# Layer 2's attention: products in column halves except the scores, five score banks, projections of four head pairs tile by tile, and new orders

## The chip, the cores and the metric

The program runs on one NeuronCore of a Trainium2 chip. Five engines work side by side, each through its own queue in order, and hand work over by semaphores: TensorE (PE; its weight loads are shown apart, as PEld), VectorE (DVE), ScalarE (ACT), GpSimd (POOL) and SyncE (SP), which starts transfers here. TensorE writes into PSUM, eight banks of 128 partitions x 512 f32 numbers. The metric is the device time of one execution in microseconds (us).

## The reference

Four layers of attention and feed-forward on x of 8 x 512 x 128, each with a layer norm before and a residual added behind. The change touches only the attention of layer 2 (16 heads of 64, S = 512):

```python
q = jnp.einsum('bsd,hpd->bhsp', x, q_w) + q_b      # x is the layer norm's result
k = jnp.einsum('bsd,hpd->bhsp', x, k_w) + k_b
v = jnp.einsum('bsd,hpd->bhsp', x, v_w) + v_b
scores = jnp.einsum('bhqp,bhkp->bhqk', q, k) / jnp.sqrt(jnp.float32(P))
attn = jax.nn.softmax(scores, axis=2)              # over the queries q, not the keys
ctx = jnp.einsum('bhqk,bhkp->bqhp', attn, v)
out = concat(ctx) @ l_w.T + l_b                    # and x = x + out
```

Since the softmax runs over the queries, its sum belongs to a key, and the kernel divides the values by it instead of the exponentials.

## The kernel before

Every engine has one list of steps for this stage, a string of letters in `Attention2.ORDER`; `order()` turns a letter and its running number into a step. The letters that matter: a `vproj`, b `kq`, c `score`, d `ctx`, e `project`, f `turn`, g `ahead` (small work for the next layer), and on DVE also h `stats`, i `low parts`, j `rows`, k `values`, l `turned`, m `add`; on ACT o `ctx out`. An engine does its steps in that order and waits on semaphores inside them. Nothing else orders the work.

The work is cut into 64 units n: block b = n // 8 of 512 tokens (one sequence), and head pair hp = n % 8. For each unit:

- `kq` (L1973), twice: keys and queries of both heads, 128 x 512, from three f16 products (high x high, low x high, high x low: `PARTS`). ACT writes the high part into `T` (L2079), DVE the low part (L2033).
- `score` (L1994), four times, one for each tile j of 128 keys: three f16 products for each of the two heads. A head has 64 rows of contraction, so the two heads use the upper and lower row half of the array ("64*128" in the profile) and write two neighbouring banks. DVE takes the row maximum of both banks at once (L2048, 1024 elements) and scales it (L2050); ACT takes two exponentials into `E` with their sums (L2087, followed by a readout of the accumulator). 
- `values`: DVE inverts the sums (L2053), POOL multiplies the values by them into `vn` (L2109).
- `ctx` (L2004), twice, each for two key tiles: f32 products with 64 columns of weights for each head, so the two heads use the left and right column half of the array ("128*64"). `ctx out` (L2095): ACT copies the bank to `cx`.
- `project` (L2014): four f32 products of 128 tokens into bank 6, which sums over the eight head pairs of a block. After the eighth, DVE adds the bank to x (`add`, L213).

`vproj` (L1983) makes the values of a block, eight pieces of 128 x 512, with three f16 products each (DVE L2041 evacuates). `kq`, `vproj` and `project` use the whole array ("128*128").

An f32 product is two MATMUL records in the trace (x8 for four products), an f16 product is one.

PSUM: banks 0 to 3 hold two scores (score j uses banks 2(j % 2) and the next), so a score waits for both exponentials of the one two before it. The other uses rotate over banks 4, 5 and 7: `self.bank` numbers them in the order of the tensor list, and `released` lets a use wait until the third before it has been evacuated. Bank 6 is the projection's. `E` has six buffers (three units), `cx` two, `T`, `vn`, `mx`, `zs` two units each.

At its start the stage still shares DVE with the layer norms of later blocks (`stats`, `rows`: L161, L164, L179). At its end the next layer waits for the last `add`.

Of the kernel before, what the change touches and what calls it, by code (L numbers as in the profile page):

```python
# [7 lines left out]
ALU = mybir.AluOpType  # L8
# [1698 lines left out]
class LowRank:  # L1707
# [45 lines left out]
    def vector(self, v):  # L1753
# [40 lines left out]
        for n, b in enumerate((0, 1, ORDER[0])):  # L1794
            v.wait_ge(k.sem("x5"), b + 1)
# [57 lines left out]
class Attention2:  # L1853
# [4 lines left out]
    def __init__(self, k, pre, low, ctx):  # L1858
# [4 lines left out]
        self.E = [loc(f"E{i}", [128, 4, 512]) for i in range(6)]  # L1863
# [3 lines left out]
        self.cx = [loc(f"cx{i}", [128, 512]) for i in range(2)]  # L1867
        uses = [u for what, x in self.order("tensor") for u in self.banks(what, x)]
        self.bank = {u: (4, 5, 7)[i % 3] for i, u in enumerate(uses)}
        self.last = {u: uses[i - 3] for i, u in enumerate(uses) if i > 2}  # L1870

    PARTS = ((0, 0), (1, 0), (0, 1))

# [6 lines left out]
            "aaaaaaaabbbbccabbacccbccbcdcdcabcbecdcdcabcbedccdcacbbecdcdcabcbecdcdcabcbecdcdcfacbecbdcdcabcbecdcdcabcbecdcd"  # L1880
            "cabcbecdcdcabcbecdcdcabcbecdcdcggacbbcdcedcacbbecdcdcggfcabecbcdcdcabcbecdcdcggcabbcdcedccabbecdcdcggacbbcdced"
            "ccabbecdcdcggacbbcdcedcabcbecdcdcfacbecbcddccabbecdcdcabcbecdcdcabcbecdcdcabcbecdcdcabcbecdcdcabcbecdcdcabcbec"
            "dcdcfacbecbdcdcabcbecdcdcabcbecdcdcabcbecdcdcabcbecdcdcabcbecdcdcabcbecdcdcabcbecdcdcfacbecbdcdcabcbecdcdcabcb"
            "ecdcdcabcbecdcdcabcbecdcdcabcbecdcdcabcbecdcdcabcbecdcdcfacbecbdcdcabcbecdcdcabcbecdcdcabcbecdcdcggggggggggggg"
            "gggacbbecdcdcabcbecdcdcabcbecdcdcabcbecdcdcabcbecdcdcgggggbcbecdcdcbbcdcecdcbbcdcecdcbbcdcecdcbbcdcecdcbbcdcec"
            "dcdcecdcdcecdedde"),
        "vector": (
            "hhaaaaaaaahhiiijiccajjjhahccihhcckihcjcjjjickicachhciickhcacjjjjhhhccikiccahhciickhhcacjjjcijckihcacjjjcjihcki"
            "caclhciihckhcacjjjcjickicacmciickcacciickcacciickcacciickcnaccickiccaciickcncalcickiccacickiccncaickicmccackii"
            "ccnacickicccackiiccnacgggggggggggckgciicacggickicggccalckiciggggccaggckiicgcacmickicggcacggickicgcacgickicgggc"  # L1890
            "acgckiiccacickiccacickiccaclickiccacickiccacmickiccacickiccacickiccacickiccacickiccacickiccaclickiccacickiccac"
            "mickiccacickiccacickiccacickiccacickiccacickiccaclickiccacickiccacmickiccacickiccacgigckiccacickiccacickiccaci"
            "ckiccacickicccickicccickicmccickicccickicccickicccickicccckccckm"),
# [12 lines left out]

    def steps(self):
# [8 lines left out]
        every["add"] = range(NB)  # L1918
# [8 lines left out]

    def banks(self, what, x):

        if what in ("kq", "vproj"):  # L1930
            return [(what, x)]
# [15 lines left out]
    def evacuated(self, p, use):  # L1947
# [15 lines left out]
    def tensor(self, p):  # L1963
        k, ps, pre, vn, E = self.k, self.k.ps, self.pre, self.vn, self.E
        ahead = self.low.tensor(p, self.bank, self.released)
        for what, x in self.order("tensor"):
            if what == "kq":
# [4 lines left out]
                for o, (q, r) in enumerate(self.PARTS):  # L1972
                    t = p.e.matmul(ps[:, self.bank[what, x], :], pre.part(("kw", "qw")[x[1]], r, slice(128 * hp, 128 * hp + 128)), halves(k, b)[q],  # L1973
                                   start=o == 0, stop=o == 2)
                t.then_inc(k.sem("kqm").h, 1)
            elif what == "vproj":
# [5 lines left out]
                for o, (q, r) in enumerate(self.PARTS):  # L1982
                    t = p.e.matmul(ps[:, self.bank[what, x], :], halves(k, b)[q][:, 128 * j:128 * j + 128],  # L1983
                                   pre.part("vw", r, slice(512 * c, 512 * c + 512)), start=o == 0, stop=o == 2)
                t.then_inc(k.sem("vproj").h, 1)
            elif what == "score":
                n, j = x
                t, at = self.T[n % 2], 2 * (j % 2)
                p.wait_ge(k.sem("E"), 2 * (4 * n + j) - 2)
                p.wait_ge(k.sem("thi"), 2 * n + 2)  # L1990
                p.wait_ge(k.sem("tlo"), 2 * n + 2)
                for o, (q, r) in enumerate(self.PARTS):
                    for hh, rows in enumerate((slice(0, 64), slice(64, 128))):
                        y = p.e.matmul(ps[:, at + hh, :], t[rows, q, 128 * j:128 * j + 128], t[rows, 2 + r, :], start=o == 0, stop=o == 2)  # L1994
                y.then_inc(k.sem("score").h, 1)
            elif what == "ctx":
# [863 lines left out]
```

## Time and profile before

| | us |
|---|---|
| median of 3 runs | 1479.46 (1477.49 to 1480.4) |
| span of the profiled execution, first to last instruction | 1470.9 |
| PE busy in it | 1406.0 (96%) |
| DVE busy | 1191.3 (81%) |
| ACT busy | 1106.2 (75%) |
| POOL busy | 284.1 (19%) |

The page gives no time of its own for the profiled execution beside the span; the median of the runs is 8.6 us above the span, which is what lies around the first and last instruction. The attention of layer 2 fills the stretch from about 567 to 1220 us of the span. Durations are those of this one execution. The end of a matmul is modelled, so times of TensorE are best read from start to start: the start of a row minus the start of the next row is what the piece took of the engine.

### The profile page before, as it was taken

To read this page: it belongs to the slowest core of one execution; us is meant where nothing else is said; L and a number is where in the kernel's file an instruction comes from. 1 tells how busy PE (TensorE), PEld (TensorE's weight loads), DVE (VectorE), ACT (ScalarE), POOL (GpSimd) and SP (SyncE) were. 2 spreads that over 40 slices of the span, in tenths; PEclk is the share of its full clock that TensorE was granted. 3 is DMA by queue.
4 is the path that set the end of the run, shared out by engine and by line. 5 is a ranking of instruction groups with operands and counts; after the bars stand their busy time and mean duration, and the time that the engine had idled before them with its cause. 6 is when DMAs were issued, how large, how long until landed. Compare 5 with 4: busy or idle time off the path is not lost.

```text
span 1470.9 us, 23734 instructions
## 1 busy us (share of the span) xinstructions
PE 1406.0 (96%) x8601; PEld 680.8 (46%) x8601; DVE 1191.3 (81%) x2559; ACT 1106.2 (75%) x2072; POOL 284.1 (19%) x239
## 2 busy tenths in 40 slices
PE   5989999999989998999999999999999999999997
PEld 4643333332248875333333333333333335555796
DVE  7699768583369979998788998888788767999997
ACT  3579888898867733788788888888888885887645
POOL 6212000000023322221111110111011112243542
PEclk9999999999999999999999999999999999999999
DMA  4176555656210001000000000000000000000000
GB/s 109 28 156 179 155 146 153 150 147 153 100 55 2 1 1 72 1 1 1 1 1 0 1 1 1 1 1 1 1 1 1 1 30 1 1 8 8 8 15 23
DMA packets 43621, 63.15 MB, mean 43 GB/s; under 512 B 5360, under 2 KB 25072, under 8 KB 43120
## 3 DMA queue, kind: packets, MB, share of 16 engines
q1 hardware_dynamic: 43504, 61.62, 15.7%
q8 instruction: 69, 1.13, 0.3%
q14 instruction: 48, 0.39, 0.1%
HBM read 54.27 MB, written 7.34 MB: 42 GB/s over the span
## 4 chain that ended last, share of the span: by engine, by line
PE 73%; DVE 15%; POOL 3%; ACT 3%; issue 2%; DMA 2%; SPq 1%; DVEq 0%; ACTq 0%
PE ps L2004 16%; PE ps L1994 13%; PE ps L525 8%; PE ps L515 7%; PE ps L1973 6%; PE ps L2014 4%; PE ps L1983 3%; DVE p6ac L2504 2%; PE ps L534 2%; POOL WA L2184 1%; PE ps L2397 1%; DVE X L213 1%; POOL WA L2188 1%; DVE st L161 1%; PE ps L448 1%
## 5 line engine op out<-in xcount | busy, mean ns | idle before, releaser
L2087 ACT ACTIVATE p4E<-ps,p4mx,p4sc 128x512 f32<-128x512 f32 x512 | 393.6, 773 | 108.3 <-DVE p4mx L2050 107.7
L2048 DVE TENSOR_REDUCE p4mx<-ps 128x2 f32<-128x1024 f32 x256 | 312.7, 1222 | 86.8 <-PE ps L1994 84.2
L2004 PE MATMUL ps<-p4E,p4vn 128*64 128x512 f32 x1024 | 248.3, 606 | 0.2 <-POOL p4vn L2109 0.2
L1994 PE MATMUL ps<-p4T 64*128 64x512 f16 x1536 | 209.9, 380 | 5.9 <-ACT p4E L2087 5.9
L2109 POOL TENSOR_TENSOR p4vn<-p4v,p4zs 128x512 f32<-128x512 f32 x64 | 66.8, 1044 | 480.3 <-DVE p4zs L2053 480.3
L752 ACT ACTIVATE p1g<-ps,WB 128x1024 f32<-128x1024 f32 x128 | 135.7, 1118 | 17.9 <-PE ps L515 17.8
L657 DVE SCALAR_TENSOR_TENSOR p1Pb<-ps,WB,p1GB 128x512 f32<-128x512 f32 x128 | 94.9, 748 | 64.1 <-PE ps L525 60.7
L515 PE MATMUL ps<-p1R,p1w1s 128*128 128x512 bf16 x512 | 131.7, 381 | 6.7 <-ACT xT L752 4.5
L1994 PEld LDWEIGHTS ps<-p4T 64*128 64x128 f16 x1536 | 54.6, 94 | 174.9 <-issue 102.9
L525 PE MATMUL ps<-p1g,WB 128*32 128x512 f32 x512 | 125.7, 599 | 0.8 <-DMA p1GB<-gscr 0.7
L525 PE MATMUL ps<-xn,WB 128*32 128x512 f32 x256 | 124.8, 599 | 0.0
L2004 PEld LDWEIGHTS ps<-p4E,p4vn 128*64 128x64 f32 x1024 | 62.4, 136 | 127.2 <-issue 125.8
L173 POOL TENSOR_TENSOR rs<-rs,cst 128x4 f32<-128x4 f32 x58 | 64.4, 1110 | 209.5 <-DVE rs L167 208.5
L1973 PE MATMUL ps<-xT,WA 128*128 128x512 f16 x384 | 101.6, 381 | 1.2 <-DVE p4T L2033 0.7
L2087 ACT ACTIVATION_READ_ACCUMULATOR p4E<-ps,p4mx,p4sc 128x1 f32 x512 | 99.9, 195 | 0.0
L2079 ACT ACTIVATE p4T<-ps,p4qkb 128x512 f16<-128x512 f32 x128 | 85.9, 684 | 12.7 <-PE ps L1973 10.1
L2033 DVE SCALAR_TENSOR_TENSOR p4T<-ps,p4qkb,p4T 128x512 f16<-128x512 f32 x128 | 91.8, 727 | 3.8 <-ACT p4T L2079 0.6
L515 PEld LDWEIGHTS ps<-p1R,p1w1s 128*128 128x128 bf16 x512 | 40.7, 98 | 114.8 <-issue 52.8
L752 ACT ACTIVATE xT<-ps,WB 128x1024 f32<-128x1024 f32 x64 | 70.0, 1117 | 21.9 <-PE ps L515 21.9
L191 ACT ACTIVATE xn<-X,sh,rs 128x128 f32<-128x128 f32 x152 | 62.1, 486 | 26.5 <-DVE sh L186 26.4
L2504 DVE SCALAR_TENSOR_TENSOR p6ac<-p6xp,WA,p6ac 128x512 f32<-128x512 f32 x94 | 79.0, 841 | 1.7
L2014 PEld LDWEIGHTS ps<-WA,p4cx 128*128 128x128 f32 x512 | 66.2, 191 | 16.3 <-issue 4.7
(369 smaller groups left out, 2508.7 us busy)
## 6 DMA issues: line engine op xcount, KB each, us to landing
p1GB<-gscr SPq DMA_DIRECT2D x128, 256.0 KB
p1R<-tscr SPq DMA_DIRECT2D x64, 128.0 KB, 5.0
tscr<-p1tp SPq DMA_DIRECT2D x24, 128.0 KB, 3.4
WA<-in_w SPq DMA_DIRECT2D x1, 2632.0 KB, 17.9
WB<-in_w SPq DMA_DIRECT2D x1, 2560.0 KB, 8.8
X<-in_x SPq DMA_DIRECT2D x8, 256.0 KB, 5.8
gscr<-p1gT SPq DMA_DIRECT2D x8, 256.0 KB, 4.7
out<-X SPq DMA_DIRECT2D x7, 256.0 KB, 2.3
```

The lines of the kernel that those rows point to most:

```text
L515: t = p.e.matmul(ps[:, ka + hh, :], self.w1s[:, 128 * ep:128 * ep + 128], self.R[b % 2][:, 2 * hp + hh, :], start=True, stop=True)
L525: p.e.matmul(ps[32 * c:32 * c + 32, bank[what, x], :], W1("w2")[:, 32 * ep:32 * ep + 32], self.gb[i % 8][:, 512 * hh:512 * hh + 512], star ...
L657: v.e.scalar_tensor_tensor(self.Pb[m % 12][:, :], ps[:, bank["comb", x], :], W1("b2")[:, half:half + 1], self.GB[n % 4][:, hh, :], ALU.add ...
L752: a.e.activation(self.gb[x % 8], ps[:, ka:ka + 2, :].rearrange("p a c -> p (a c)"), ACT.Gelu, bias=k.Wt(1, "b1")[:, ep:ep + 1]).then_inc(k ...
L1973: t = p.e.matmul(ps[:, self.bank[what, x], :], pre.part(("kw", "qw")[x[1]], r, slice(128 * hp, 128 * hp + 128)), halves(k, b)[q], start=o ...
L1994: y = p.e.matmul(ps[:, at + hh, :], t[rows, q, 128 * j:128 * j + 128], t[rows, 2 + r, :], start=o == 0, stop=o == 2)
L2004: t = p.e.matmul(ps[64 * hh:64 * hh + 64, self.bank["ctx", n], :], vn[n % 2][:, j, 64 * hh:64 * hh + 64], E[2 * (n % 3) + hh][:, j, :], st ...
L2014: t = p.e.matmul(ps[:, 6, 128 * j:128 * j + 128], self.cx[x % 2][:, 128 * j:128 * j + 128], k.Wt(4, "lw")[:, 128 * hp:128 * hp + 128], sta ...
L2033: v.e.scalar_tensor_tensor(t[:, 2 * c + 1, :], ps[:, self.bank["kq", x], :], pre.qkb[:, 1 - c, hp:hp + 1], t[:, 2 * c, :], ALU.add, ALU.su ...
L2048: v.e.tensor_reduce(m, ps[:, at:at + 2, :], AX, ALU.max).then_inc(v.own.h, v.one())
L2087: a.e.activation(self.E[2 * (n % 3) + hh][:, j, :], ps[:, at + hh, :], ACT.Exp, bias=self.mx[i][:, j, hh:hh + 1], scale=pre.sc[:, 1, 0:1], ...
L2504: t = v.e.scalar_tensor_tensor(ac[:, :], src, et[:, m:m + 1], ac[:, :], ALU.mult, ALU.add)
```

## The change

In words, part by part:

1. **Column halves.** `kq`, `vproj` and `project` make each product as two, for weight columns 0 to 63 and 64 to 127, with the same moving operand (`HALVES`). The number of matmuls doubles, each has 64 columns. `ctx` had that form already, the scores keep their row halves.
2. **Five score banks.** Scores go round banks 0 to 4 (`SCORE`, `pair`). Pair m takes places 2m and 2m + 1 of the round, so every fifth pair sits in banks 4 and 0: there DVE takes two maxima of 512 instead of one of 1024. ACT takes the exponential of the older place first. A score now waits for `E` >= 2m - 3 instead of 2m - 2: one exponential less.
3. **Projections.** Bank 6 no longer sums over eight head pairs. For the first 60 steps a projection x takes token tile j = x % 4 of four head pairs (4g to 4g + 3, g = x // 4), with both column halves, into a quarter of a bank out of the rotation, and DVE adds that tile, 128 x 128, to x (`add`, 60 times). The last four head pairs go as before, pair by pair into one bank, with one add of 512.
4. **Buffers.** `E` four instead of six (exponentials of unit n wait for the `ctx` of n - 2, not n - 3), `cx` eight instead of two. The rotating uses, projections among them now, have banks 5, 6, 7.
5. **New orders** for all engines. In the tensor list 248 runs of scores become 182 (72 of them two long); DVE's list has the layer norm's steps later, and the values' pieces of block 0 between the first scores instead of ahead of them.

```diff
+    def pair(self, m):
+        first, second = self.SCORE[2 * m % 5], self.SCORE[(2 * m + 1) % 5]
+        return ((first, second), (0, 1)) if first < second else ((second, first), (1, 0))
...
-        self.E = [loc(f"E{i}", [128, 4, 512]) for i in range(6)]
+        self.E = [loc(f"E{i}", [128, 4, 512]) for i in range(4)]
-        self.cx = [loc(f"cx{i}", [128, 512]) for i in range(2)]
+        self.cx = [loc(f"cx{i}", [128, 512]) for i in range(8)]
-        self.bank = {u: (4, 5, 7)[i % 3] for i, u in enumerate(uses)}
+        self.bank = {u: (5, 6, 7)[i % 3] for i, u in enumerate(uses)}
+    SCORE = (0, 1, 2, 3, 4)
+    HALVES = (slice(0, 64), slice(64, 128))
...
     ORDER = {
         "tensor": (
-            "aaaaaaaabbbbccabbacccbccbcdcdcabcbecdcdcabcbedccdcacbbecdcdcabcbecdcdcabcbecdcdcfacbecbdcdcabcbecdcdcabcbecdcd"
+            "bbbacbacccabcabcacaaaacabdcdcabcdccadacbbbccddccabbcdcdccaebcdcdcbabccdbcgdbceecfcbbcdcdaccdcdacbbeccabbcdcdce"
...
                 for o, (q, r) in enumerate(self.PARTS):
-                    t = p.e.matmul(ps[:, self.bank[what, x], :], pre.part(("kw", "qw")[x[1]], r, slice(128 * hp, 128 * hp + 128)), halves(k, b)[q],
-                                   start=o == 0, stop=o == 2)
+                    w = pre.part(("kw", "qw")[x[1]], r, slice(128 * hp, 128 * hp + 128))
+                    for at in self.HALVES:
+                        t = p.e.matmul(ps[at, self.bank[what, x], :], w[:, at], halves(k, b)[q], start=o == 0, stop=o == 2)
...
-                t, at = self.T[n % 2], 2 * (j % 2)
-                p.wait_ge(k.sem("E"), 2 * (4 * n + j) - 2)
+                t, (banks, _) = self.T[n % 2], self.pair(4 * n + j)
+                p.wait_ge(k.sem("E"), 2 * (4 * n + j) - 3)
...
             elif what == "project":
+                if x < 60:
+                    g, j = divmod(x, 4)
+                    p.wait_ge(k.sem("cx"), 4 * g + 4)
+                    self.released(p, (what, x))
+                    for n in range(4 * g, 4 * g + 4):
+                        for at in self.HALVES:
+                            t = p.e.matmul(ps[at, self.bank[what, x], 0:128], self.cx[n % 8][:, 128 * j:128 * j + 128][:, at], lw(n),
+                                           start=n == 4 * g, stop=n == 4 * g + 3)
...
+                if high == low + 1:
+                    v.e.tensor_reduce(m, ps[:, low:low + 2, :], AX, ALU.max).then_inc(v.own.h, v.one())
+                else:
+                    v.e.tensor_reduce(m[:, 0:1], ps[:, low, :], AX, ALU.max).then_inc(v.own.h, v.one())
+                    v.e.tensor_reduce(m[:, 1:2], ps[:, high, :], AX, ALU.max).then_inc(v.own.h, v.one())
...
-                a.wait_ge(k.sem("ctx"), n - 2)
+                a.wait_ge(k.sem("ctx"), n - 1)
```

**TensorE in the middle of the stage.** One unit before, from its order. L1994 are scores, L2004 ctx, L1983 vproj, L1973 kq, L2014 project; in the changed kernel these are L2011, L2021, L2001, L1990 and L2034.

```order
1185 L1994 MATMUL ps<-p4T 128x512 x6
1186 L1983 MATMUL ps<-WA,xT 128x512 x3
1187 L1973 MATMUL ps<-xT,WA 128x512 x3
1188 L1994 MATMUL ps<-p4T 128x512 x6
1189 L1973 MATMUL ps<-xT,WA 128x512 x3
1190 L2014 MATMUL ps<-WA,p4cx 128x128 x4
1191 L1994 MATMUL ps<-p4T 128x512 x6
1192 L2004 MATMUL ps<-p4E,p4vn 64x512 x4
1193 L1994 MATMUL ps<-p4T 128x512 x6
1194 L2004 MATMUL ps<-p4E,p4vn 64x512 x4
```

And in the changed kernel, at a like place:

```order
1163 L2011 MATMUL ps<-p4T 128x512 x12
1164 L1990 MATMUL ps<-xT,WA 64x512 x12
1165 L2021 MATMUL ps<-p4E,p4vn 64x512 x4
1166 L2011 MATMUL ps<-p4T 128x512 x12
1167 L2021 MATMUL ps<-p4E,p4vn 64x512 x4
1168 L2034 MATMUL ps<-WA,p4cx 64x128 x8
1169 L2011 MATMUL ps<-p4T 128x512 x12
1170 L1990 MATMUL ps<-xT,WA 64x512 x12
1171 L2021 MATMUL ps<-p4E,p4vn 64x512 x4
1172 L2011 MATMUL ps<-p4T 128x512 x12
```

Before, each score (x6) stands alone between pieces of another shape; now two scores often stand together (x12), and what is between them is all of 64 columns. An x12 of L1990 is two kq steps, an x8 of L2034 one tile's projection.

**VectorE at the start of the stage.** Before (L161, L164, L179 are layer norms of later blocks, L2041 evacuates vproj, L2033 kq, L2048 the maxima):

```order
691 L2041 SCALAR_TENSOR_TENSOR p4v<-ps,p4sc,WA 128x512 x8
692 L161 BN_STATS st<-X 128x6
693 L164 BN_AGGR mv<-st 128x2
694 L161 BN_STATS st<-X 128x6
695 L164 BN_AGGR mv<-st 128x2
696 L167 TENSOR_SCALAR rs<-mv 128x4
697 L2033 SCALAR_TENSOR_TENSOR p4T<-ps,p4qkb,p4T 128x512 x3
698 L179 TENSOR_SCALAR xn<-X,mv,rs 128x128
699 L2033 SCALAR_TENSOR_TENSOR p4T<-ps,p4qkb,p4T 128x512
700 L2048 TENSOR_REDUCE p4mx<-ps 128x2
```

And now (L2069, L2061 and L2078 are the same three; L2080 and L2081 the two single maxima, L2083 the scaling):

```order
691 L2061 SCALAR_TENSOR_TENSOR p4T<-ps,p4qkb,p4T 128x512 x3
692 L2069 SCALAR_TENSOR_TENSOR p4v<-ps,p4sc,WA 128x512
693 L2078 TENSOR_REDUCE p4mx<-ps 128x2
694 L2083 TENSOR_SCALAR p4mx<-p4mx,p4sc 128x2
695 L2061 SCALAR_TENSOR_TENSOR p4T<-ps,p4qkb,p4T 128x512
696 L2078 TENSOR_REDUCE p4mx<-ps 128x2
697 L2083 TENSOR_SCALAR p4mx<-p4mx,p4sc 128x2
698 L2080 TENSOR_REDUCE p4mx<-ps 128x1
699 L2081 TENSOR_REDUCE p4mx<-ps 128x1
700 L2083 TENSOR_SCALAR p4mx<-p4mx,p4sc 128x2
```

The first maximum stands third instead of behind eight evacuations and two norms.

**TensorE at the end of the stage.** In the changed kernel, to the next layer's first product (L2387); L2042 is the projection pair by pair, L197 a turn of the next layer's input:

```order
1318 L2034 MATMUL ps<-WA,p4cx 64x128 x16
1319 L2011 MATMUL ps<-p4T 128x512 x6
1320 L197 MATMUL ps<-cst,xn 128x128 x4
1321 L2011 MATMUL ps<-p4T 128x512 x6
1322 L2042 MATMUL ps<-WA,p4cx 64x128 x16
1323 L2021 MATMUL ps<-p4E,p4vn 64x512 x16
1324 L2042 MATMUL ps<-WA,p4cx 64x128 x16
1325 L2387 MATMUL ps<-cst,p5g 8x128 x8
```

Before, one ctx, one project, two ctx and one project follow the last score; now two projects, four ctx and two projects do.

## Rows read from the trace of the kernel before

**Rows 1.** Page, busy time of each engine (share of the span) and instructions.
```profile
PE 1406.0 (96%) x8601; PEld 680.8 (46%) x8601; DVE 1191.3 (81%) x2559; ACT 1106.2 (75%) x2072; POOL 284.1 (19%) x239
```
**Rows 2.** Busy time of each engine by stretch of the span; PEclk is the granted clock.
```profile
567.00:627.00 60.00, 50.43 (x280) 18.19 (x281) 56.28 (x121) 40.90 (x94) 14.40 (x13) 0.97 0.12 45
627.00:1195.00 568.00, 567.45 (x3295) 208.69 (x3293) 475.23 (x789) 470.88 (x1104) 75.03 (x73) 1.00 0.01 3
1195.00:1219.30 24.30, 21.50 (x124) 8.33 (x120) 10.31 (x17) 14.27 (x35) 2.50 (x3) 1.00 0.00 1
```
**Rows 3.** What PE waited for, 567 to 1221 us: total, times, longest.
```profile
PE ps L1994 <- ACT p4E L2087: 5.9, 3, 3.0
PE ps L2014 <- ACT p4cx L2095: 2.5, 2, 1.9
PE ps L1983 <- DVE p4v L2041: 1.6, 1, 1.6
PE ps L1983 <- DVE X L213: 1.5, 1, 1.5
```
**Rows 4.** PE in order of time, one unit: start us, us, line, array part, xcount.
```profile
905.12 0.81 PE L1973 MATMUL ps<-xT,WA 128*128 128x512 f16 x3
905.87 0.82 PE L1994 MATMUL ps<-p4T 64*128 64x512 f16 x6
906.62 0.82 PE L1973 MATMUL ps<-xT,WA 128*128 128x512 f16 x3
907.28 1.05 PE L2014 MATMUL ps<-WA,p4cx 128*128 128x128 f32 x8
908.26 0.82 PE L1994 MATMUL ps<-p4T 64*128 64x512 f16 x6
909.01 1.94 PE L2004 MATMUL ps<-p4E,p4vn 128*64 128x512 f32 x8
910.88 0.82 PE L1994 MATMUL ps<-p4T 64*128 64x512 f16 x6
```
**Rows 5.** PE in order of time, two scores together.
```profile
616.85 1.47 PE L1994 MATMUL ps<-p4T 64*128 64x512 f16 x12
618.25 1.94 PE L2004 MATMUL ps<-p4E,p4vn 128*64 128x512 f32 x8
```
**Rows 6.** PE's weight loads in order of time, one ctx step.
```profile
899.22 0.20 PEld L2004 LDWEIGHTS ps<-p4E,p4vn 128*64 128x64 f32 x4 [0.42 <-issue]
899.70 0.14 PEld L2004 LDWEIGHTS ps<-p4E,p4vn 128*64 128x64 f32 x2 [0.29 <-issue]
```
**Rows 7.** PE in order of time in layer 0, four column groups.
```profile
104.32 0.61 PE L525 MATMUL ps<-p1g,WB 128*32 128x512 f32 x3
...
104.75 0.61 PE L525 MATMUL ps<-p1g,WB 128*32 128x512 f32 x3
```
**Rows 8.** Groups of DVE by line: xcount, busy us, mean ns.
```profile
L2048 DVE TENSOR_REDUCE p4mx<-ps 128x2 f32<-128x1024 f32 x256 | 312.7, 1222 | 86.8 <-PE ps L1994 84.2
L2050 DVE TENSOR_SCALAR p4mx<-p4mx,p4sc 128x2 f32<-128x2 f32 x256 | 58.7, 229 | 9.1
L1751 DVE TENSOR_REDUCE p5nrm<-ps 128x1 f32<-128x512 f32 x5 | 3.4, 684 | 0.0
L213 DVE TENSOR_TENSOR X<-X,ps 128x512 f32<-128x512 f32 x11 | 7.4, 684 | 7.7 <-PE ps L2014 7.5
L1558 DVE TENSOR_TENSOR p2on<-ps,p2rd 128x128 f32<-128x128 f32 x32 | 6.8, 276 | 0.0
```
**Rows 9.** All engines in order of time, the stage's end.
```profile
1208.10 0.82 PE L1994 MATMUL ps<-p4T 64*128 64x512 f16 x6
1212.65 1.16 PE L2014 MATMUL ps<-WA,p4cx 128*128 128x128 f32 x8 [1.86 <-ACT p4cx L2095]
1213.74 3.65 PE L2004 MATMUL ps<-p4E,p4vn 128*64 128x512 f32 x16
1218.08 1.16 PE L2014 MATMUL ps<-WA,p4cx 128*128 128x128 f32 x8 [0.69 <-ACT p4cx L2095]
```

More of the change, by code:

```diff
@@ L1917, in steps @@
         every |= {what: later for what in ("rstd", "turn", "turned")}
-        every["add"] = range(NB)
+        every["add"] = range(61)
         return every
@@ L1926, in order, with added @@
             yield kind, next(left[kind])
+    @staticmethod
+    def added(b):
+        return min(8 * b + 8, 61)
+    def pair(self, m):
+        first, second = self.SCORE[2 * m % 5], self.SCORE[(2 * m + 1) % 5]
+        return ((first, second), (0, 1)) if first < second else ((second, first), (1, 0))
     def banks(self, what, x):
         if what in ("kq", "vproj"):
+            return [(what, x)]
+        if what == "project" and x <= 60:
             return [(what, x)]
@@ L1955, in evacuated @@
             p.wait_ge(k.sem("cx"), x + 1)
+        elif what == "project":
+            p.wait_ge(k.sem("x5"), x + 1)
         elif what == "squares":
@@ L1982, in tensor @@
                 for o, (q, r) in enumerate(self.PARTS):
-                    t = p.e.matmul(ps[:, self.bank[what, x], :], halves(k, b)[q][:, 128 * j:128 * j + 128],
-                                   pre.part("vw", r, slice(512 * c, 512 * c + 512)), start=o == 0, stop=o == 2)
+                    xs = halves(k, b)[q][:, 128 * j:128 * j + 128]
+                    for at in self.HALVES:
+                        t = p.e.matmul(ps[at, self.bank[what, x], :], xs[:, at], pre.part("vw", r, slice(512 * c, 512 * c + 512)), start=o == 0, stop=o == 2)
                 t.then_inc(k.sem("vproj").h, 1)
@@ L1992, in tensor @@
                 for o, (q, r) in enumerate(self.PARTS):
-                    for hh, rows in enumerate((slice(0, 64), slice(64, 128))):
-                        y = p.e.matmul(ps[:, at + hh, :], t[rows, q, 128 * j:128 * j + 128], t[rows, 2 + r, :], start=o == 0, stop=o == 2)
+                    for hh, rows in enumerate(self.HALVES):
+                        y = p.e.matmul(ps[:, banks[hh], :], t[rows, q, 128 * j:128 * j + 128], t[rows, 2 + r, :], start=o == 0, stop=o == 2)
                 y.then_inc(k.sem("score").h, 1)
@@ L2081, in scalar @@
                 n, j = x
[L2082 removed]
+                i, (banks, turn) = n % 2, self.pair(4 * n + j)
                 a.wait_ge(k.sem("mx"), 4 * n + j + 1)
[L2084 removed]
+                a.wait_ge(k.sem("ctx"), n - 1)
                 a.wait_ge(k.sem("vn"), n - 1)
[L2086 to L2087 removed]
+                for hh in turn:
+                    a.e.activation(self.E[2 * i + hh][:, j, :], ps[:, banks[hh], :], ACT.Exp, bias=self.mx[i][:, j, hh:hh + 1], scale=pre.sc[:, 1, 0:1],
                                    accum_out=self.zs[i][:, j, hh:hh + 1]).then_inc(k.sem("E").h, 1)
```

87 lines of the change are left out of this document (50 added, 37 removed).

## The prediction

> **What bounds the kernel now.** I read the page's busy times first: PE is busy for 96% of the span, DVE for 81%, ACT for 75% [rows 1]. Such shares are averages, so the next view is the busy time by stretch. In layer 2's attention, from 627 to 1195 us, PE is busy 567.45 of 568.00 us, DVE 475.23, ACT 470.88 [rows 2]. Nothing that DVE or ACT does there is paid for; each us saved on PE is a us of the kernel, as long as DVE keeps some of its 93 us of cover. The two ends of the stage are different: in the 60 us from 567 PE is idle for 9.6 while DVE is busy for 56.28, and in the last 24.3 us PE is idle for 2.8 [rows 2]. The waits name who it was: the start waits for exponentials, evacuations of the values and the previous layer's last adds, the end for `cx` [rows 3]. So there are three questions: what does PE's own work cost after the change, what becomes of some 12 us of idle time at the ends, and do new waits appear in the middle.
>
> PE's work is read from start to start. A kq step takes 906.62 to 907.28 = 0.66 us when another whole-array step follows, but 905.12 to 905.87 = 0.75 when a score follows; a score takes 0.75 [rows 4], and two together take 616.85 to 618.25 = 1.40 [rows 5]. So 0.65 is the work (three slots of 0.216) and each change of the array's shape costs 0.09 to 0.10. A ctx step takes 1.87 [rows 4], while a row of 16 records is 3.65 long and one of 8 is 1.94 [rows 9, 5]: 1.71 of work and 0.16 for the two changes. The weight loads show where the extra 0.05 is: the first pair of loads is followed by the next after 0.48, not after the 0.43 of the later ones [rows 6, 7]. A project takes 907.28 to 908.26 = 0.98: 0.89 of work, 0.09 for the change [rows 4].
>
> **Changes of shape.** In the built order of before I count 508 changes in this stage: 116 from a score to ctx, 124 back, 132 from a score to the whole array, 124 back, 12 others. Priced as above: 116 x 0.15 + 124 x 0.10 + 132 x 0.10 + 124 x 0.09 + 12 x 0.15 = 17.4 + 12.4 + 13.2 + 11.2 + 1.8 = 56.0 us. After it there are 366, since all but scores and a few small products have columns of 64 and scores stand in 182 runs: 64 from a score to ctx, 104 from a score to the new halves, 174 back, 24 others. No row shows f16 halves entered from a score. They cost 0.10 if they behave as kq did, 0.15 if as ctx does; I take 0.12, nearer the f16 rows. Then 64 x 0.15 + 104 x 0.12 + 174 x 0.10 + 24 x 0.12 = 9.6 + 12.5 + 17.4 + 2.9 = 42.4 us. The term is -13.6 us (-10.5 to -15.7).
>
> **The products in halves.** `kq` and `vproj` are 192 steps of three products, now of three pairs. If the halves of a pair run side by side, the step stays at 0.65 and the term is 0; if not, each takes another 0.65 and it is +125 us. The nearest rows say side by side: the ctx pairs (8 records of 512 columns in 1.71, so 0.43 for two) and, in layer 0, four column groups of an f32 product in 0.43 [rows 6, 7]. And f16 in two row halves does six in 0.65 [rows 4]. I take 0. Each product now needs two loads. They are hidden behind the pair before, as in the ctx rows, where loads are busy for 0.14 out of 0.43 [rows 6]; uncovered they would cost at most 192 x 3 x 0.14 = 81 us, the same upper case in kind.
>
> The Trainium skill, TensorEngine Tiling (Array Packing), Gotcha 2: Feature Incompatibilities, speaks against this edit: column tiling gives up the fast weight load, which the f16 loads of the whole array may use. By TensorE: Matmul & The Clock Gate, LDWEIGHTS (loading the stationary operand), a load of 64 columns would then be an estimated 53 ns, so two are 107 ns behind a slot of 216. That would leave the sum where it is.
>
> `project` had 512 records of 128 columns, 0.11 each [rows 4]; now it has 1024, in pairs. If the pair takes 0.11 the term is 0. The densest that any row shows is a matmul each 0.108 us (six in 0.65, or four in 0.43) [rows 4, 7]; if that is a limit on issue and not on columns, a step of 16 takes 1.73 instead of 0.89, and 64 steps cost +54 us. Rows 7 have four products in one 0.43, each of which streams for that long, so they are bound by their columns; I take 0.
>
> **DVE and ACT.** 60 adds of 128 x 128 at 0.276 instead of seven of 512 at 0.684: +11.8 us. 51 of the 256 maxima are taken as two of 0.684 instead of one of 1.222: +7.4 [rows 8]. Together +19 on DVE, taken at 0 for the kernel, because it lies in the 93 us in which DVE waited for PE; with the cover gone it would be +19. ACT's work does not change (0).
>
> **The start.** The waits for exponentials there [rows 3] follow from the four banks: a score needs both exponentials of the second before it, and that is a chain of 0.17 to the matmul's end, 1.22 maximum, 0.23 scaling and two exponentials of 0.77: 3.2 us. Where the list of before leaves less than that, PE waits: I count five scores, all in the first units, short by 8.1 in sum. With the fifth bank one exponential is enough, 2.4 us, and the new list leaves less in four places, short by 2.6. DVE, which sets this stretch, also has less in front of it: up to the sums of unit 6 it does 11 `stats` and 16 `rows` less than before. But two units of `E` instead of three, and values' evacuations that still must come ahead of the first ctx, take a part of it back. I take -4 us, between 0 and -7.
>
> **The end.** Before, the last score starts at 1208.10, and the ctx that needs it at 1213.74, so 5.0 us after the score's 0.65 [rows 9]. In that time PE did one ctx and one project and waited 1.9; at the end it waited 0.7 for `cx` [rows 9]. Now two projects (1.9) and two ctx (3.4) lie there, 5.3 us, and a project covers the last `cx`: -2.5 us (0 to -3).
>
> **New waits in the middle.** With three banks for five uses a unit instead of four, and orders that keep less distance, PE can come to wait. I compared the distances in PE's work. From a unit's last score to its ctx: median 12.4 before, 8.6 now, never under 5.3, needed 5.0. From the queries to their first score: median 10.9 before, 5.8 now, smallest 3.1 but for the first unit, needed about 2.4 with a maximum ahead in DVE's queue. From a bank's evacuation step to its next use, after ctx under 1.6 us in a tenth of the cases. Before, the distances were so long that the middle had 0.5 us of waits [rows 2]; now they are near the need, and every wait delays an engine with nothing to spare. I take +5 us; the bounds are 0 and, at 0.5 us in each of 64 units, +32.
>
> **Sum.** -13.6 + 0 + 0 - 4 - 2.5 + 5 = -15.1 us on a span of 1470.9. The median lies 8.6 above the span and I let that stand: 1479.5 - 15 = 1464.5 us. Its own range, from the terms' bounds without the rivals: 1456 to 1473.
>
> **Rivals.**
> 1. *The middle fills with waits.* Three rotating banks and `E` two units deep: a ctx waits for `vn`, exponentials wait for the ctx, the next scores for the exponentials, each unit. For it: a need of 5.0 against a smallest distance of 5.3, and DVE at (475 + 19) / 555 = 89% in the middle. Against it: the direct distances are all above the need. Price: 0.5 us a unit, 32 us, in place of my 5: 1464.5 + 27 = 1491.5. It decides the sign from 0.31 us a unit (20 us) on.
> 2. *Little of the shape's price goes.* Entering the halves costs 0.15 and waits take some 15 us: -10.5 - 2 - 1 + 15, about 1481, no change to be told.
> 3. *Issue-bound projections.* If records cannot come faster than 0.108 us, +54: about 1518. A smaller form of it, 0.062 us a record, gives 16 x 0.062 = 0.99 for 0.89, +6.4, still faster than before: 1471.
> 4. *The f16 halves do not run side by side*: +125, 1590.
>
> For the smaller form of the third, the Trainium skill, TensorE: Matmul & The Clock Gate, Wait — 56ns, not 53.3ns?, gives 62 ns for each MATMUL when it is decoded in microcode, and about 25 ns otherwise. By the second figure the pair of 107 ns stays bound by its columns.
>
> **Chances.** Forecast and near it 0.74; rival 1 0.11; rival 2 0.08; rival 3 in its large form 0.03, in its small one inside the forecast's; rival 4 0.04. A change under 0.2% (3 us) cannot be told from none. Faster by more 0.76, within 0.07, slower 0.17. The range takes in the forecast's own and most of rival 1: 1454 to 1488.
>
> **What would show it.** A kq step in halves between others of 64 columns takes 0.65 from start to start, a tile's projection 0.86 to 0.9, and two scores together 1.40: if a kq step takes 1.3, rival 4 holds, if a projection takes 1.7, rival 3. The middle of the stage shows PE with 5 to 8 us of waits; over 25 us is rival 1, and the waits' view then names `vn`, `cx`, `X` or `E`. At the end the ctx after the last score follows without a wait. The stage's DVE busy time grows by about 19 us. I am wrong on the main term if PE is as full as before and the stage not shorter.

## The result and the profile after

| | before | after |
|---|---|---|
| median of 4 runs, us | 1478.47 (1474.32 to 1480.4) | 1453.26 (1451.28 to 1454.46) |
| span of the profiled execution, us | 1470.9 | 1452.0 |
| stage: first product of the attention to the next layer's first product, us | 651.2 | 628.6 |

The ratio is 0.9836 (95% interval 0.9816 to 0.9855): faster by 1.6%, 24 us. The time came out 11 us below the predicted 1464.5 and 0.7 below the 1454 at the low end of the stated range; the kernel before, measured again beside it, was itself 1.0 below the 1479.46 from which the forecast started. The stage is the cleanest measure, since it leaves out what differs from execution to execution ahead of it: the attention began at 568.8 us in the profiled execution before, at 575.7 in the one after, and between 570.8 and 575.8 in the kernels of the experiments, which differ in this stage only. It lasted from 568.80 to 1220.01 before and from 575.68 to 1204.31 after. So in the profile the stage gave 22.6 us, the part behind it another 3.1 (250.8 to 247.7), and the part ahead of it took 6.9 back.

PE in order of time in the changed kernel, one stretch of the middle; columns as in [rows 4]:

```profile
900.42 1.94 PE L2021 MATMUL ps<-p4E,p4vn 128*64 128x512 f32 x8
902.19 0.82 PE L1990 MATMUL ps<-xT,WA 128*64 128x512 f16 x6
902.94 0.82 PE L2011 MATMUL ps<-p4T 64*128 64x512 f16 x6
903.69 1.97 PE L2034 MATMUL ps<-WA,p4cx 128*64 128x128 f32 x32
905.49 0.82 PE L2001 MATMUL ps<-WA,xT 128*64 128x512 f16 x6
906.24 0.82 PE L2011 MATMUL ps<-p4T 64*128 64x512 f16 x6
906.99 0.84 PE L2001 MATMUL ps<-WA,xT 128*64 128x512 f16 x6
```

Start to start: ctx before kq 1.77, where it took 1.87 before a score [rows 4]; kq and vproj in halves before a score 0.75, as on the whole array; two tile projections 1.80, so 0.90 each. No product became slower by its halves. What is gone is the change of shape between ctx and its neighbours.

Busy time by stretch (PE, PEld, DVE, ACT, POOL, granted clock, DMA), the three stretches of the stage, to be read against [rows 2]:

```profile
575.68:635.00 59.32, 55.73 (x406) 19.33 (x406) 55.50 (x103) 47.26 (x108) 8.69 (x8) 1.00 0.12 45
635.00:1180.00 545.00, 543.26 (x4164) 212.97 (x4164) 485.34 (x899) 460.00 (x1084) 79.43 (x76) 1.00 0.00 1
1180.00:1204.31 24.31, 23.52 (x215) 11.43 (x210) 13.83 (x26) 15.87 (x38) 3.13 (x3) 1.00 0.13 44
```

PE is still full in the middle (1.7 us idle of 545; DVE has 60 us of idle time left), idle for 3.6 us at the start instead of 9.6 (1.5 of which lay ahead of the stage's first product) and for 0.8 at the end. The waits of PE in the stage, as in [rows 3]:

```profile
PE ps L2011 <- ACT p4E L2130: 3.5, 5, 1.6
PE ps L1990 <- DVE X L213: 1.5, 1, 1.5
PE ps L2001 <- DVE p4T L2061: 0.9, 2, 0.5
PE ps L2387 <- DVE X L213: 0.8, 1, 0.8
PE ps L2001 <- DVE p4v L2069: 0.4, 1, 0.4
```

In the kernel before, the same view has four more lines under those of [rows 3]:

```profile
PE ps L2343 <- DVE X L213: 0.8, 1, 0.8
PE ps L1973 <- DVE p4T L2033: 0.7, 1, 0.7
PE ps L1973 <- DVE xT L2065: 0.4, 1, 0.4
PE ps L2004 <- POOL p4vn L2109: 0.2, 1, 0.2
```

In both kernels the 1.5 for X lies ahead of the stage's first product and the 0.8 for X at its end. From that first product on, the waits before add up to 12.1 us: 8.2 at the start (5.9, 1.6 and 0.7), 0.4 in the middle and 3.5 at the end. After, they are 5.6: 3.6 at the start (2.3 of the 3.5 for exponentials, 0.9 and 0.4), 1.3 in the middle (the other three waits for exponentials) and 0.8 at the end. The wait for `cx` at the end is gone. Taking waits off the stage leaves PE's own work: 639.1 us before, 623.0 after, 16.1 less.

Not all of the 16.1 is the array's shape. At the stage's start the granted clock (seventh column) fell to 0.50 in the kernel before, after waits of 3.0 and 2.1 us, and PE's pieces took about twice as long:

```profile
593.60:597.00 3.40, 3.40 (x12) 0.81 (x12) 2.77 (x6) 2.40 (x8) 0.00 (x0) 0.50 0.00 0
```

```profile
593.04 0.96 PE L1973 MATMUL ps<-xT,WA 128*128 128x512 f16 x3
593.94 1.46 PE L1994 MATMUL ps<-p4T 64*128 64x512 f16 x6
595.33 2.75 PE L2004 MATMUL ps<-p4E,p4vn 128*64 128x512 f32 x8
598.01 0.82 PE L1994 MATMUL ps<-p4T 64*128 64x512 f16 x6
```

Start to start these are 0.90, 1.39 and 2.68 where 0.75, 0.75 and 1.87 are usual: 1.6 us more. In the changed kernel the longest wait at the start is 1.6 and the clock stays at 1.00 there. So 1.6 of the 16.1 us are the clock and 14.5 are left.

The DVE groups that the prediction priced, against [rows 8] (in the stage DVE is busy for 554.7 us, where it was for 540.7):

```profile
L2078 DVE TENSOR_REDUCE p4mx<-ps 128x2 f32<-128x1024 f32 x205 | 249.7, 1218 | 29.3 <-PE ps L2011 28.3
L2080 DVE TENSOR_REDUCE p4mx<-ps 128x1 f32<-128x512 f32 x51 | 35.0, 687 | 10.7 <-PE ps L2011 10.6
L2095 DVE TENSOR_TENSOR X<-X,ps 128x128 f32<-128x128 f32 x60 | 16.5, 277 | 2.2 <-PE ps L2034 1.7
```

### The profile page after: what moved, and what is told of

Its sections match the earlier page's. It is cut to its first block, busy times and chain, and to the rows that moved or that the text cites. A ratio compares the mean times of both kernels' runs of the same rounds, so it can differ in the third digit from the quotient of the medians.

```text
span 1452.0 us, 25984 instructions
## 1 busy us (share of the span) xinstructions
PE 1385.7 (95%) x9655; PEld 690.1 (48%) x9689; DVE 1205.6 (83%) x2663; ACT 1103.4 (76%) x2072; POOL 283.7 (20%) x239
## 3 DMA queue, kind: packets, MB, share of 16 engines
q8 instruction: 77, 1.26, 0.4%
## 4 chain that ended last, share of the span: by engine, by line
PE 65%; DVE 18%; DMA 6%; POOL 4%; ACT 3%; issue 3%; SPq 2%; DVEq 0%; ACTq 0%
PE ps L2021 15%; PE ps L2011 12%; PE ps L1990 6%; PE ps L525 6%; PE ps L515 4%; PE ps L2034 4%; DVE p6ac L2548 3%; PE ps L2001 3%; DMA p1GB<-gscr 3%; DMA tscr<-p1tp 1%; POOL WA L2228 1%; PE ps L534 1%; PE ps L2483 1%; DVE X L213 1%; PE ps L448 1%
## 5 line engine op out<-in xcount | busy, mean ns | idle before, releaser
L2078 DVE TENSOR_REDUCE p4mx<-ps 128x2 f32<-128x1024 f32 x205 | 249.7, 1218 | 29.3 <-PE ps L2011 28.3
L2021 PE MATMUL ps<-p4E,p4vn 128*64 128x512 f32 x1024 | 243.0, 599 | 0.2
L2011 PE MATMUL ps<-p4T 64*128 64x512 f16 x1536 | 199.3, 379 | 3.8 <-ACT p4E L2130 3.5
L515 PE MATMUL ps<-p1R,p1w1s 128*128 128x512 bf16 x478 | 124.8, 381 | 11.7 <-ACT xT L752 4.5
L2011 PEld LDWEIGHTS ps<-p4T 64*128 64x128 f16 x1536 | 58.2, 94 | 157.1 <-ACT p4E L2130 86.7
L2021 PEld LDWEIGHTS ps<-p4E,p4vn 128*64 128x64 f32 x1024 | 66.8, 136 | 115.6 <-issue 104.9
L1990 PE MATMUL ps<-xT,WA 128*64 128x512 f16 x768 | 102.8, 383 | 1.5 <-DVE X L213 1.5
L2130 ACT ACTIVATION_READ_ACCUMULATOR p4E<-ps,p4mx,p4sc 128x1 f32 x512 | 103.2, 202 | 0.0
L2061 DVE SCALAR_TENSOR_TENSOR p4T<-ps,p4qkb,p4T 128x512 f16<-128x512 f32 x128 | 94.1, 741 | 6.0 <-ACT p4T L2122 5.3
L2083 DVE TENSOR_SCALAR p4mx<-p4mx,p4sc 128x2 f32<-128x2 f32 x256 | 64.5, 252 | 9.0
```

Source lines behind the costliest of these rows:

```text
L515: t = p.e.matmul(ps[:, ka + hh, :], self.w1s[:, 128 * ep:128 * ep + 128], self.R[b % 2][:, 2 * hp + hh, :], start=True, stop=True)
L1990: t = p.e.matmul(ps[at, self.bank[what, x], :], w[:, at], halves(k, b)[q], start=o == 0, stop=o == 2)
L2011: y = p.e.matmul(ps[:, banks[hh], :], t[rows, q, 128 * j:128 * j + 128], t[rows, 2 + r, :], start=o == 0, stop=o == 2)
L2061: v.e.scalar_tensor_tensor(t[:, 2 * c + 1, :], ps[:, self.bank["kq", x], :], pre.qkb[:, 1 - c, hp:hp + 1], t[:, 2 * c, :], ALU.add, ALU.su ...
L2078: v.e.tensor_reduce(m, ps[:, low:low + 2, :], AX, ALU.max).then_inc(v.own.h, v.one())
L2130: a.e.activation(self.E[2 * i + hh][:, j, :], ps[:, banks[hh], :], ACT.Exp, bias=self.mx[i][:, j, hh:hh + 1], scale=pre.sc[:, 1, 0:1], acc ...
```

## The experiments

Times are ratios to runs of the kernel before on the same chip; where parts of the stage are compared I use its length in the profiled execution: 651.2 us before, 628.6 after. That is one execution of each kernel, but the stage repeats well: the last two projections start 625.89 us behind its first product in the changed kernel, and 625.87 behind it in the last experiment, whose kernel is the same up to there.

**Column halves alone.** The kernel before with each product of `kq`, `vproj` and `project` written as in the change:

```diff
-                    t = p.e.matmul(ps[:, self.bank[what, x], :], pre.part(...), halves(k, b)[q], start=o == 0, stop=o == 2)
+                    w = pre.part(...)
+                    for at in self.HALVES:
+                        t = p.e.matmul(ps[at, self.bank[what, x], :], w[:, at], halves(k, b)[q], start=o == 0, stop=o == 2)
```

> The kernel before with kq, vproj and project in column halves, and nothing else of the change (old orders, four score banks, bank 6 for the projection). Theory (the gain is the number of shape changes times 0.1 to 0.16 us, and the halves have no speed of their own): scores still stand in 248 runs, 506 changes against 508, so no gain, -1 to +3 us against before. Rival (products in halves are faster in themselves): -8 us or more. In its trace a kq step between others is 0.65 to 0.67 from start to start.

Measured: ratio 1.0 (0.9985 to 1.0015), stage 650.6. PE in order of time in this kernel:

```profile
909.88 0.81 PE L1976 MATMUL ps<-xT,WA 128*64 128x512 f16 x6
910.62 0.82 PE L1997 MATMUL ps<-p4T 64*128 64x512 f16 x6
911.37 0.84 PE L1976 MATMUL ps<-xT,WA 128*64 128x512 f16 x6
912.04 1.04 PE L2018 MATMUL ps<-WA,p4cx 128*64 128x128 f32 x16
913.02 0.82 PE L1997 MATMUL ps<-p4T 64*128 64x512 f16 x6
```

A kq step takes 0.67 before a projection, the projection 0.98 before a score: the halves run side by side and give nothing by themselves (0.6 us in the stage is too little to be called a gain). With a score between nearly all pieces there is no change of shape that they could save.

**The whole array with the new orders.** The reverse: the changed kernel with the three kinds on the whole array again.

```diff
-                    for at in self.HALVES:
-                        t = p.e.matmul(ps[at, self.bank[what, x], :], w[:, at], halves(k, b)[q], start=o == 0, stop=o == 2)
+                    t = p.e.matmul(ps[:, self.bank[what, x], :], w, halves(k, b)[q], start=o == 0, stop=o == 2)
```

> The changed kernel with kq, vproj and project on the whole array again, its orders, banks and buffers kept. Theory: 449 changes of shape against 366, 83 more, those between ctx and the whole array, at 0.10 to 0.15: +8 to +12 us against the changed kernel, 1461 to 1465. Rival (the gain is the orders and buffers alone): within 2 us of the changed kernel.

Measured: ratio 0.9912 (0.9882 to 0.9941), median 1462.3, stage 639.5: 10.8 us longer than the change, with waits as in it (3.9 for exponentials). 83 changes of shape more cost 10.8 us, 0.13 each. So the halves are worth 10.8 us in the new orders and next to nothing in the old ones; orders, banks, buffers and projections without them are worth 11.8. Of these 11.8, 6.0 are listed waits (12.1 to 6.1) and 1.6 the clock at the start, which stays at 1.00 here too; 4.2 are left for 59 changes of shape fewer. No run takes the orders, the buffers or the projections by tiles alone.

**Four score banks.**

```diff
-    SCORE = (0, 1, 2, 3, 4)
+    SCORE = (0, 1, 2, 3)
...
-                p.wait_ge(k.sem("E"), 2 * (4 * n + j) - 3)
+                p.wait_ge(k.sem("E"), 2 * (4 * n + j) - 2)
```

> The changed kernel with four score banks (a score waits for both exponentials of the second before it), orders kept; no maximum is split in two. Theory (the orders can stand scores in twos only because the fifth bank asks for one exponential less): 45 scores have less than the 3.2 us that both exponentials need, short by 17 us in sum against 2.6 with five, so PE waits for exponentials in the middle too: +8 to +16 us. Rival (DVE's load is what matters, and it falls by 7 us without the split maxima): no slower than the changed kernel, or faster.

Measured: ratio 1.0197 (1.0171 to 1.0223), 1504.9 us, stage 679.7: 51 us more, three times the upper end of what was expected. PE's waits:

```profile
PE ps L2011 <- ACT p4E L2130: 41.3, 85, 2.3
```

The direction and the waiter are as the theory has them, the size is not: 85 waits came where I counted 45. I had compared only the direct way from a score to its exponential; on ACT the exponentials also stand behind kq's high parts and the copies of ctx. That this is the reason is argued from the lists, and no run separates it. (The view counts a wait from a matmul's modelled end, 0.17 us behind the start of the next piece where nothing waits: a score's row is 0.82 long and its work 0.65. Listed are 42.5 us in all, 36.9 more than in the change; 79 more waits at 0.17 are 13, and together these are 50 of the 51.) With the same letters and 366 changes of shape, the fifth bank is worth more in these orders than the whole change.

**The first eight vproj ahead.** The first eight letters a of the tensor list moved to its front, on DVE to behind the first two h (the start of the tensor list is shown):

```diff
-            "bbbacbacccabcabcacaaaacabdcdcabcdccadacbbbccddccabbcdcdccaeb
+            "aaaaaaaabbbcbcccbcbccacabdcdcabcdccadacbbbccddccabbcdcdccaeb
...
```

> The changed kernel with the first eight vproj ahead of all else on PE and their evacuations ahead on DVE, as before; the rest of the orders kept. Theory (part of the gain is the start of the stage, where the first maximum no longer stands behind eight evacuations): +3 to +5 us, all as waits in the first 60 us of the stage. Rival (the start gains by the layer norm's steps put off, not by this): within 1 us.

Measured: ratio 0.9871 (0.984 to 0.9903), median 1457.1, stage 632.7: 4.1 us longer. The medians are 3.8 us apart, within the intervals of the two ratios, so it is the stage that shows it. The listed waits grew by 1.9 us (5.5 for exponentials and 1.2 for kq's low part, where 3.5, 0.9 and 0.4 stood). The other 2.2 are in no listed wait. They are the clock, which after waits of 1.2 and 2.2 us fell at the start:

```profile
585.50:592.50 7.00, 6.59 (x30) 1.53 (x30) 5.01 (x10) 5.80 (x15) 0.15 (x1) 0.56 0.01 2
```

Four pieces in a row, from 585.70 to 591.33, take 1.39 to 1.43 from start to start where 0.75 is usual: 2.6 us more. So that order at the start is worth 4 us in this execution, about half by waits and half by the clock.

**All maxima split.** The test of DVE's cover: two maxima of 512 for every pair.

```diff
-                if high == low + 1:
+                if False:
```

> The changed kernel with every pair's maxima taken as two of 512 (256 pairs instead of 51), so DVE has 205 x 0.14 = 29 us more to do and each score's way to its exponential is 0.14 longer. Theory (PE bounds the middle, DVE has 60 us of idle time there in the changed kernel, 485 busy of 545): most of it is hidden, +2 to +8 us. Rival (since DVE is busy for 89%, it binds as much as PE): +20 us or more, and so the split maxima of the change cost their 7 us.

Measured: median 1451.1, ratio 0.9835 (0.981 to 0.986), the same as the change; stage 629.9, 1.3 longer, no wait more. But the doubled cost was smaller than I had said. DVE in order of time:

```profile
904.25 0.67 DVE L2080 TENSOR_REDUCE p4mx<-ps 128x1 f32<-128x512 f32 x1
904.84 0.68 DVE L2081 TENSOR_REDUCE p4mx<-ps 128x1 f32<-128x512 f32 x1
905.55 0.23 DVE L2083 TENSOR_SCALAR p4mx<-p4mx,p4sc 128x2 f32<-128x2 f32 x1
```

From the first maximum to the scaling it is 1.30 us; one maximum of 1024 in the changed kernel takes 1.22 plus the gap, 1.26 from start to start in the kernel before. A split costs 0.04 us, not 0.14: the second maximum starts 0.59 behind the first, whose record is 0.67 long. DVE's busy time in the stage says much the same: 565.9 us against 554.7, 0.05 for each of the 205 more splits. So the splits of the change are as good as free, and 11 us more of DVE's work cost the stage 1.3; how much more it could take, this does not say.

**The end of before filled.** 19 small products in the two waits, nothing else:

```diff
             elif what == "project":
                 b, hp = divmod(x, 8)
+                if x >= 62:
+                    p.wait_ge(k.sem("E"), 510)
+                    k.busy(p, 0, (14, 5)[x - 62])
```

> The kernel before with 19 small bf16 products (128 x 256, results unused) put into PE's two waits at the stage's end, 14 ahead of the second last project and 5 ahead of the last. Theory (before, those waits and the next layer's first one let the granted clock fall to 1.2 GHz for some 7 us behind the stage's end, which costs the 2 to 3 us by which the part behind the stage is longer before than after): clock 1.00 in the 15 us behind the stage's end, that part 2 to 3 us shorter than 250.9, the stage itself unchanged within 0.3 us: -2 to -3 us in all. Rival (the part behind the stage is shorter for another reason, other adds or another phase): no change there, or the stage longer by the products' 2 us.

Measured: ratio 0.9996 (0.9978 to 1.0014), too small to be told in the times; in the profile the stage is 651.2 as before and the part behind it 248.8, 2.0 less. The granted clock (seventh column) behind the stage before:

```profile
1220.01:1225.00 4.99, 2.85 (x15) 1.65 (x16) 4.87 (x34) 4.64 (x15) 3.36 (x4) 1.00 0.00 0
1225.00:1230.00 5.00, 5.00 (x21) 4.04 (x20) 4.97 (x22) 4.12 (x8) 2.20 (x2) 0.51 0.01 3
1230.00:1235.00 5.00, 5.00 (x38) 5.00 (x38) 4.96 (x18) 2.13 (x5) 2.49 (x2) 0.81 0.00 0
```

with the end filled:

```profile
1224.20:1229.20 5.00, 2.86 (x16) 1.61 (x16) 4.90 (x34) 4.69 (x15) 3.39 (x4) 1.00 0.00 0
1229.20:1234.20 5.00, 5.00 (x28) 4.30 (x27) 4.96 (x22) 4.21 (x9) 2.15 (x2) 0.66 0.01 3
```

and in the changed kernel:

```profile
1204.31:1209.30 4.99, 2.85 (x15) 1.64 (x16) 4.88 (x34) 4.65 (x15) 3.36 (x4) 1.00 0.00 0
1209.30:1214.30 5.00, 5.00 (x42) 4.47 (x41) 4.97 (x22) 4.11 (x8) 2.20 (x2) 1.00 0.00 0
```

In the same 5 us PE finishes 21 records at half the clock and 42 at full. The theory expected 1.00 throughout; the clock was still low for part of a stretch. And the 2.0 us cannot be put down to the filled waits: the next experiment's kernel has the end of before with both waits in it (1.9 and 0.7 for `cx`), and behind its stage the clock was as with the end filled:

```profile
1322.19:1327.19 5.00, 5.00 (x27) 4.26 (x26) 4.97 (x22) 4.21 (x9) 2.19 (x2) 0.66 0.02 3
```

Over all kernels but the last experiment's, the part behind the stage goes with the clock: 250.8 and 250.9 us where it was 0.51 and then 0.81 (before, halves alone), 248.6 to 248.9 where it was 0.66 or 0.67 in one stretch of 5 us (whole array, four banks, vproj first, all maxima split, the filled end, four buffers), and 247.7 where it stayed at 1.00 (the change). What decides how long the clock is low is not shown: of the three kernels with both waits for `cx` two had the long form and one the short, and the kernel with all maxima split has the waits of the change and yet had the short form. So of the 3.1 us no part is shown to be the change's.

**Before with four buffers of exponentials.**

```diff
-        self.E = [loc(f"E{i}", [128, 4, 512]) for i in range(6)]
+        self.E = [loc(f"E{i}", [128, 4, 512]) for i in range(4)]
...
-                a.wait_ge(k.sem("ctx"), n - 2)
+                a.wait_ge(k.sem("ctx"), n - 1)
```

> The kernel before with four buffers of exponentials instead of six (exponentials of unit n wait for the ctx of n - 2), as the changed kernel has, and nothing else. It tells whether the orders of before need the third unit. Theory (the lists and the depth of the buffers belong together): in the list of before the second ctx step of unit n - 2 stands behind the second score of unit n, so the exponentials of each unit wait for it and hold back the third score by about 1.9 us: 64 x 1.9 = 120 us more, between 80 and 150. Rival (depth is slack that nobody uses): within 5 us of before.

Measured: ratio 1.0622 (1.0594 to 1.065), +91 us, within what the theory expected. PE's waits:

```profile
PE ps L1994 <- ACT p4E L2087: 93.7, 55, 3.0
```

The old list needs its third unit: PE waits 55 times, 1.7 us on average. In it the second ctx of unit n - 2 stands behind two scores of unit n in 47 of 62 units, behind one in the others. In the new list it stands behind one score in 41 units, ahead of all in 21, and never behind two; PE's waits for exponentials in the middle are three, 1.3 us together. That the new lists lose nothing by two units is read from this; no run gives them back the third.

**The price of a change of shape.** The changed kernel with extra products behind the last projection. `rows` are two row halves (L2060), `columns` two f16 column halves (L2064), `whole` one f16 product on the whole array (L2067), `wide` two f32 column halves (L2071):

```diff
+        for kind in (rows, columns, whole, wide):
+            for _ in range(12):
+                kind()
+        for kind in (columns, whole, wide):
+            for _ in range(12):
+                rows()
+                kind()
```

> The changed kernel with extra products behind the last projection, results unused: 12 steps each of row halves (R), f16 column halves (C), whole array (F) and f32 column halves (W), each kind together; then R and C, R and F, R and W in turns, 12 times each. Only the trace is read. Theory: together R, C and F take 0.216 a step and W 0.43; a turn of R and C or R and F takes 0.43 + two changes of 0.10 = 0.62 to 0.64, a turn of R and W 0.65 + 0.25 = 0.90. Rival (a pair of f16 column halves costs more than the whole array in itself, or its entry 0.15 as for f32): C together over 0.23, or R and C in turns 0.05 longer than R and F. The time grows by 13.0 for the first part and by 26 for the second.

Measured, in order of time:

```profile
1198.90 2.76 PE L2060 MATMUL ps<-p4T 64*128 64x512 f16 x24
1201.59 2.78 PE L2064 MATMUL ps<-p4T 128*64 128x512 f16 x24
1204.30 2.76 PE L2067 MATMUL ps<-p4T 128*128 128x512 f16 x12
1207.00 10.52 PE L2071 MATMUL ps<-p4E,p4vn 128*64 128x512 f32 x48
...
1217.77 0.41 PE L2064 MATMUL ps<-p4T 128*64 128x512 f16 x2
1218.11 0.39 PE L2060 MATMUL ps<-p4T 64*128 64x512 f16 x2
1218.43 0.41 PE L2064 MATMUL ps<-p4T 128*64 128x512 f16 x2
...
1226.32 0.39 PE L2067 MATMUL ps<-p4T 128*128 128x512 f16 x1
1226.65 0.39 PE L2060 MATMUL ps<-p4T 64*128 64x512 f16 x2
1226.97 0.39 PE L2067 MATMUL ps<-p4T 128*128 128x512 f16 x1
...
1234.42 0.39 PE L2060 MATMUL ps<-p4T 64*128 64x512 f16 x2
1234.74 1.08 PE L2071 MATMUL ps<-p4E,p4vn 128*64 128x512 f32 x4
1235.75 0.39 PE L2060 MATMUL ps<-p4T 64*128 64x512 f16 x2
```

Twelve steps of a kind take 2.69 to 2.71 us with the change at their end, so 0.216 each for the three f16 kinds. In turns, a step of halves and one of rows take 0.66, whole array and rows 0.64 to 0.65, f32 halves and rows 1.33. (A wide step is four records, 0.87 in a run; I had priced it as two, so both the 0.90 for the turn and the growth of 13 and 26 us were wrong. The parts took 18.6 and 31.6.) The two changes of a turn are 0.23, 0.21 and 0.25: 0.10 to leave and 0.10 to enter, and 0.02 more to enter f16 halves, 0.05 more to enter f32 halves.

## Why the prediction was right or wrong

| term | predicted | measured |
|---|---|---|
| changes of shape | -13.6 (-10.5 to -15.7) | -14.5 in PE's work |
| products in halves, f16 and projections | 0 | 0 |
| start of the stage | -4 (0 to -7) | -4.6 in waits, -1.6 by the clock |
| end of the stage | -2.5 (0 to -3) | -2.7 |
| new waits in the middle | +5 (0 to +32) | +0.9 |
| behind the stage | not in the sum | -3.1 |

The measured terms of the stage add up to its 22.6 us (rounded). They are what one execution of each kernel shows, where the sum was -15.1.

**Changes of shape: right.** The price of f16 halves entered from a score, the one that no row showed, was taken as 0.12 and is 0.10 + 0.02. 142 changes fewer and 14.5 us less work are 0.10 a change, and the term was 0.9 us too small. The 14.5 is an attribution by subtraction (stage less listed waits less clock); for 83 of the changes the whole-array run shows it directly, at 0.13 each.

**The halves: right, with a better reason than I gave.** They cost nothing and are worth nothing in the old list; together with scores in twos they are worth 10.8 us. The rule that column tiling gives up the fast weight load (the Trainium skill, TensorEngine Tiling (Array Packing), Gotcha 2: Feature Incompatibilities) has no price here that the trace shows: a run of f16 halves steps takes the 0.216 of the whole array. The projections fit too: 32 records in 1.80 are 0.056 a record, so neither 0.108 nor 0.062 a record was a limit.

**The start and the end: right, and a little too small.** The listed waits of the start were 5.9, 1.6 and 0.7 before and are 2.3, 0.9 and 0.4 after, 4.6 less; at the end `cx`'s 2.5 and a wait of 0.2 for `vn` are gone. What the prediction left out is that the start's waits also cost clock: 1.6 us before, nothing after. Where the eight vproj stand is worth 4.1 us of the 6.2 in the execution that tests it.

**New waits: the term that was sized wrong.** The prediction said that PE "can come to wait" in the middle, and took +5. The listed waits there went from 0.4 to 1.3 us (its idle time from 0.5 to 1.7), all of them for exponentials and none for `vn`, `cx`, X or a rotating bank. That the distances in the new lists are nearer to the need was right, and the need was met all the same. Four score banks show how near: the same lists with one exponential more to wait for lose 51 us, where my count of distances gave 17. So that count was no measure of the waits, and the +5 was not worked out from it: it was a guess between 0 and an assumed 0.5 us a unit. This is the largest miss in the stage, 4.1 us.

**What was not in the sum.** The part behind the stage was 3.1 us shorter in the profile, with a clock that did not fall; the runs do not show that the change brings this about. And I took what lies around the span as 8.6 us, by median less span. Each of the four runs after has 1.9 us around its span, so the 8.6 was mostly the difference between the profiled execution before and a middling one. It did no harm, since the forecast took it for both kernels. The range was also added up loosely: by the terms' own bounds its low end is 1479.5 - 15.7 - 7 - 3 = 1453.8, not 1456, and 1488 does not reach the 1491.5 of the first rival. That the measured 1453.3 lies at the low end comes from misses of one sign: 4.1 in the middle, 3.1 behind the stage, 2.2 at the start, 0.9 in the changes of shape and 0.2 at the end.

DVE's busy time in the stage grew by 14.0 us, not 19: at the 0.05 us a split that the run with all maxima split shows, 51 of them are 3 us, not 7.4. Little of it can show in the time: PE waits for DVE nowhere in the middle, and with all maxima split 11 us more of it cost 1.3.

Of the rivals, the first (waits of 0.5 us a unit) did not happen, and the two on halves and projections that are not side by side are out: a kq step of halves takes 0.66 to 0.67 and a tile's projection 0.90 us. The second (entry at 0.15 and 15 us of waits) is out as well: 0.12 and 0.9.

## What to carry to other kernels

Where TensorE is full, count the changes of array shape in its order, price them from start to start, and judge an edit by the changes it takes away: the halves gave nothing until the orders stood scores in twos. A list written for a tight schedule and the depth of the buffers under it belong together; one bank less cost 51 us here, one unit of buffers less 91. And read how much more an instruction costs from start to start: two neighbours overlap, and a split that their durations price at 0.14 us cost 0.04. Look at the granted clock before you call what is left of a stretch without its waits the engine's work: here it held 1.6 us of 16.1, and the whole rest of another comparison.

## What the runs showed of the hardware

- A change of the array's shape (row halves, column halves, whole array) costs TensorE about 0.10 us (in turns of rows and whole array a turn takes 0.64 to 0.65 us where its two steps of 0.216 are 0.43), and entering column halves 0.02 (f16) or 0.05 (f32) more.
- Two f16 products in column halves that read the same moving operand run side by side: 0.216 us for both, as one on the whole array.
- Short waits cost clock, not in the same way each time. At the stage's start the granted clock fell for part of the first 60 us (0.94 or 0.97 over them) in the six kernels whose longest wait there was 2.2 to 3.0 us, and stayed at 1.00 in the four where it was 1.6. Behind the stage, after waits of 1.9, 0.7, 0.8 and 2.1 us within some 14 us, it was 0.51 for 5 us and 0.81 for the next in two kernels, and 0.66 in one stretch of 5 us in a third; with 0.8 and 2.1 as the long ones it was 0.66 or 0.67 in one stretch in five kernels and stayed at 1.00 in the changed kernel.
- At half the clock a score takes 1.39 us from start to start instead of 0.75, a ctx step 2.68 instead of 1.87 (the clock was low for part of it).
- Two maxima of 128 x 512 from PSUM take 1.30 us on DVE to the start of the next instruction, one of 128 x 1024 takes 1.26.
